# Masked queries by a GpSimd multiply instead of four DMAs, and the high query copies of the stack issued by ScalarE

## The chip, the cores and the metric

The kernel runs on one core of a Trainium2 chip. The metric is the time on the device in microseconds, lower is better. The core has five engines, each with its own list of instructions in a fixed order: TensorE (PE: matmuls), VectorE (DVE), ScalarE (ACT), GpSimd (POOL) and SyncE (SP), which here only issues DMAs. They wait for each other by semaphores. Every time is from a run on the chip or from a profile of one execution.

## The reference

A cross-attention layer and a feed-forward layer with 4-bit quantization, over a batch of 16. Inputs are x (16 x 224 x 512) and a context (16 x 750 x 512).

```python
def _L0_xattn_ref(q, k, v, Wq, bq, Wk, bk, Wv, bv, Wo, bo):
    qh, kh, vh = proj(q, Wq, bq), proj(k, Wk, bk), proj(v, Wv, bv)   # 16 heads of 32
    scores = jnp.einsum('bhqd,bhkd->bhqk', qh, kh) / math.sqrt(D_K)
    attn = jax.nn.softmax(scores, axis=-1)
    out = jnp.einsum('bhqk,bhkd->bhqd', attn, vh)
    return out.transpose(0, 2, 1, 3).reshape(B, -1, D_MODEL) @ Wo.T + bo

x = x + _L0_xattn_ref(_layernorm(x), ctx_1024, ctx_1024, ...)
gate, y = fp4_linear(ln, w_gate), fp4_linear(ln, w_up)               # ln = _layernorm(x)
x = x + fp4_linear(jax.nn.silu(gate) * y, w_down)
```

fp4_linear quantizes both operands in blocks of 16 and dequantizes them again before the product.

## The kernel before

Two stages follow each other: attention over all batches (the first 1650 us of the profile), then the feed-forward layer. The change lies in the attention.

The attention works through 64 slots, four per batch: a slot is a group t of 4 heads (HG = 4, 32 rows each, together 128 partitions) of one batch. Products are made exact by splitting each operand into a high part that TensorE takes whole and a low rest, and adding three products (PASSES, line 41).

For a group these steps are made, two slots ahead of its scores: the projected keys "k" (two halves) and queries "q" come from TensorE into a PSUM bank (lines 419 to 441); ScalarE copies the high part with the bias into k_part or q_part (lines 541 to 552), VectorE makes the low part (k_lo, q_lo, lines 621 to 637). There are two buffers of each by parity of t, only k_low is single.

One slot ahead, TensorE makes 16 "max" matmuls (line 473): the queries of one head against 375 keys each, whose row maximum VectorE takes (line 614). Since k_high holds 4 heads on its 128 partitions, the query operand must be zero outside the 32 rows of its head. It is q_masked, 128 x 4 x 224, whose block j holds the queries' high part on the rows of head j and zeros elsewhere. The zeros are written once at the start (line 727); the rows of the heads are copied for each group by four DMAs from q_part (line 788). The first max matmul waits for them (line 471). The negated maxima are transposed by TensorE ("shift", line 477) and copied by ScalarE into the last four rows of qstack (line 575).

For the scores a stack is made per head, so that one matmul over 100 rows does the three products and the shift: kstack holds the head's keys high, high, low and a row of ones, qstack the queries high, low, high and the shift. SyncE issues the copies: four for the low keys (line 796), then for each of the four heads two of high keys (line 802) and three of queries (line 805), 24 in all. The first score matmul of the group waits for all (lines 482 to 484).

Order: slot_units (line 177) gives every unit of work of a slot a place on a scale in which the 12 score matmuls of the slot stand at 0 to 11 (each a pair of matmuls, with an exponential on ScalarE of 128 x 448, line 539), and sorts. Each engine walks through the same sorted list and does what of each unit is its own, so an engine that waits holds up all its later units. Two score banks alternate: score n + 2 waits for exponential n. The places around the change, for group g + 1 in slot g: the low key copies 0.1, the other stack copies 0.12, max from 0.15 on, shift at about 9 and 11. For group g + 2: q at 7.12, 7.37, 6.6, 6.01 in slots 0 to 3, mask_q 0.05 after it. In slot 0 SyncE also loads the next batch's context and x at 2.6 (1500 and 448 KB, lines 773 and 777). In slot 2 ScalarE and VectorE split that context (ctx, places 0.15, 0.15, 1.88 and 2.49, lines 570 and 648) and the transposed x (0.38, 3.49). In slots 0, 1 and 3 VectorE quantizes a share of the feed-forward weights in 11 small steps (quantize_step, line 814); at places 7 to 10 these are steps with one or two SBUF inputs of 128 x 352 (lines 844 to 853).

The batches 1 to 14 are a loop on the engines (line 393), whose turn lies ahead of slot 0.

## Time and profile before

| | |
|---|---|
| Median of 3 runs | 2426.59 us (2416.27 to 2426.79) |
| The profiled execution | 2425.06 us, span 2423.2 us |
| TensorE busy (weight loads 1885.2) | 2240.0 us, 92% |
| VectorE busy | 1764.5 us, 73% |
| ScalarE busy | 844.4 us, 35% |
| GpSimd busy | 92.0 us, 4% |
| DMA, mean share of 16 engines | 29.8% on the queue of SyncE |
| Mean granted clock of TensorE | 0.969 of full speed |

The span is from the first to the last instruction, the time of an execution is slightly longer. Busy time doesn't count DMA issues: an engine that issues one is occupied and not busy. The clock is what the chip granted TensorE; 1.00 is 2.4 GHz and 0.50 is 1.2 GHz. A wait in the lists is idle time of an engine ahead of an instruction, with what ended it; "issue" is idle time that nothing the profile shows has ended.

### The profile page before, as it was taken

The numbers are of one execution on the slowest core, as the hardware profiler recorded it, in microseconds if no ns is written. First come the engines' busy times: TensorE is split into PE (matmuls) and PEld (weight loads), VectorE is DVE, ScalarE is ACT, GpSimd is POOL, SyncE is SP. The second block draws the span as 40 slices with busy tenths as digits, with TensorE's granted clock in tenths as the row PEclk, the third lists the DMA queues.
The fourth block names the chain that finished last, engine by engine and source line by source line (L and its number), as shares of the span: only waits on it lengthen the run. The fifth ranks groups of instructions, "written<-read, shape, count | busy, mean of one in ns | idle before, by whom it ended". The sixth has DMA issues, their size and how long they took to land. (4 is left out here: it accounts for less than half of the span.)

```text
span 2423.2 us, 50583 instructions
## 1 busy us (share of the span) xinstructions
PE 2240.0 (92%) x17444; PEld 1885.2 (78%) x17444; DVE 1764.5 (73%) x3102; ACT 844.4 (35%) x1677; POOL 92.0 (4%) x164
## 2 busy tenths in 40 slices
PE   4989899999998999999899999996799999999998
PEld 4778787787877877778778787864678888888887
DVE  4767667676666766757667676655899999999986
ACT  3444344443443434444344444434111111111111
POOL 0000000000000000000000000000000000000000
PEclk9999999999999999999999999998899999999999
DMA  4343434434334343443434434335000001010000
GB/s 152 107 120 80 120 89 115 118 89 117 94 110 120 83 117 90 114 123 81 117 90 114 123 82 117 92 89 163 31 27 30 36 26 39 26 39 26 35 18 27
DMA packets 136290, 204.74 MB, mean 84 GB/s; under 512 B 33872, under 2 KB 84560, under 8 KB 133568
## 3 DMA queue, kind: packets, MB, share of 16 engines
q1 hardware_dynamic: 136128, 202.22, 29.8%
q8 instruction: 146, 2.39, 0.4%
q14 instruction: 16, 0.13, 0.0%
HBM read 75.67 MB, written 23.33 MB: 41 GB/s over the span
## 5 line engine op out<-in xcount | busy, mean ns | idle before, releaser
L614 DVE TENSOR_REDUCE row_max<-max_bank 112x1 f32<-112x376 f32 (+1 forms) x1024 | 524.8, 542 | 478.0 <-PE max_bank L473 473.5
L539 ACT ACTIVATE probs<-score_bank 125x448 f32<-125x448 f32 x768 | 404.1, 542 | 315.2 <-PE score_bank L488 307.2
L473 PE MATMUL max_bank<-k_high,q_masked 128*112 128x376 f32 (+1 forms) x1024 | 321.1, 361 | 68.3 <-DMA q_masked<-q_part 55.4
L488 PE MATMUL score_bank<-qstack,kstack 100*128 100x224 f32 x1536 | 300.6, 282 | 27.8 <-issue 23.9
L488 PEld LDWEIGHTS score_bank<-qstack,kstack 100*128 100x128 f32 x1536 | 264.6, 191 | 60.0 <-issue 47.8
L473 PEld LDWEIGHTS max_bank<-k_high,q_masked 128*112 128x112 f32 x1024 | 163.9, 180 | 121.8 <-DMA q_masked<-q_part 52.8
L503 PE MATMUL pv_bank<-probs,values 125*32 125x224 f32 x3072 | 234.9, 379 | 9.2 <-ACT probs L539 9.2
L509 PE MATMUL pv_bank<-probs,ones 125*32 125x224 f32 x3072 | 232.5, 376 | 0.0
L1145 ACT ACTIVATE f_act_gate<-gate_bank 128x512 f32<-128x512 f32 (+1 forms) x84 | 47.3, 563 | 516.5 <-PE up_bank L1100 516.5
L1100 PE MATMUL gate_bank<-ffn_gate_hi,f_xqt 128*128 128x512 f32 (+1 forms) x672 | 218.9, 387 | 8.1 <-DVE f_xqt L1206 8.1
L447 PE MATMUL proj_bank<-wv_hi,ctx_hi 128*128 128x256 f32 x768 | 221.7, 289 | 4.3 <-DVE wo_lo L693 4.3
L447 PE MATMUL proj_bank<-wv_hi,ctx_lo 128*128 128x256 f32 x768 | 216.8, 282 | 0.0
L447 PE MATMUL proj_bank<-wv_lo,ctx_hi 128*128 128x256 f32 x768 | 216.7, 282 | 0.0
L1124 PE MATMUL down_bank<-ffn_down_hi,f_hqt 128*128 128x512 f32 x616 | 206.2, 401 | 6.6 <-DVE f_hqt L1222 6.6
L1100 PE MATMUL up_bank<-ffn_up_hi,f_xqt 128*128 128x512 f32 (+1 forms) x672 | 212.2, 377 | 0.0
L547 ACT ACTIVATE k_high<-proj_bank,biases 128x376 fp32r<-128x376 f32 (+1 forms) x128 | 73.5, 574 | 358.6 <-PE proj_bank L427 358.6
L427 PE MATMUL proj_bank<-ctx_hi,wk_hi 128*128 128x376 f32 (+1 forms) x512 | 176.2, 344 | 20.5 <-DVE ctx_lo L648 20.5
L427 PE MATMUL proj_bank<-ctx_lo,wk_hi 128*128 128x376 f32 (+1 forms) x512 | 173.9, 340 | 0.0
L427 PE MATMUL proj_bank<-ctx_hi,wk_lo 128*128 128x376 f32 (+1 forms) x512 | 172.6, 337 | 0.0
L447 PEld LDWEIGHTS proj_bank<-wv_hi,ctx_hi 128*128 128x128 f32 x768 | 147.7, 192 | 4.6 <-DVE wo_lo L693 4.6
L1100 PEld LDWEIGHTS gate_bank<-ffn_gate_hi,f_xqt 128*128 128x128 f32 x672 | 126.3, 189 | 27.9 <-DVE f_xqt L1206 8.5
L509 PEld LDWEIGHTS pv_bank<-probs,ones 125*32 125x32 f32 x3072 | 105.3, 116 | 53.5 <-issue 12.0
(119 smaller groups left out, 4035.5 us busy)
## 6 DMA issues: line engine op xcount, KB each, us to landing
kstack<-k_high SPq DMA_DIRECT2D x512, 93.8 KB, 2.2
ctx_raw<-in_ctx SPq DMA_DIRECT2D x16, 1500.0 KB, 7.0
kstack<-k_low SPq DMA_DIRECT2D x256, 93.8 KB, 2.2
qstack<-q_part SPq DMA_DIRECT2D x768, 28.0 KB, 1.9
ffn_quant<-fw_share SPq DMA_DIRECT2D x48, 176.0 KB, 1.9
fw_raw<-ffn_quant SPq DMA_DIRECT2D x33, 256.0 KB, 4.1
xn<-in_x SPq DMA_DIRECT2D x16, 448.0 KB, 8.0
q_masked<-q_part SPq DMA_DIRECT2D x256, 28.0 KB, 1.9
```

The lines of the kernel that those rows point to most:

```text
L427: last = nc.tensor.matmul(out[:, 0:hi - lo], w_hi_lo[W_K][ws][:, c, g * P:(g + 1) * P], ctx_part[cs][:, c, lo:hi], start=(n == 0), stop=(n ...
L447: last = nc.tensor.matmul(out[:, 0:256], ctx_part[cs][:, c, kt * KW:kt * KW + P], w_hi_lo[W_V][ws][:, c, half * 256:(half + 1) * 256], sta ...
L473: nc.tensor.matmul(out[0:QH, 0:hi - lo], q_masked[t % 2][:, j, half * QH:(half + 1) * QH], k_part[t % 2][0][:, lo:hi], start=True, stop=Tr ...
L488: last = nc.tensor.matmul(score_bank[j % 2][:, k * SQ:(k + 1) * SQ], kstack[t % 2][0:STK, j, kt * KW:kt * KW + P], qstack[t % 2][:, j, :], ...
L503: last = nc.tensor.matmul(pv_bank[t % 2][j * DK:(j + 1) * DK, 0:SQ], values[:, t % NG // 2, kt, col:col + DK], probs[p][:, j, k, :], start ...
L509: last = nc.tensor.matmul(pv_bank[t % 2][j * DK:(j + 1) * DK, SQ:2 * SQ], ones[0:KW, :], probs[p][:, j, k, :], start=False, stop=(kt == KT ...
L539: nc.scalar.activation(probs[p][:, j, :, :], score_bank[j % 2][0:KW, 0:2 * SQ].rearrange("p (k q) -> p k q", k=2), ACT.Exp, scale=float(DK ...
L547: nc.scalar.activation(k_part[t % 2][0][:, lo:hi], src[:, 0:hi - lo], ACT.Identity, bias=biases[:, 1, t % NG:t % NG + 1]).then_inc(hi_done ...
L614: nc.vector.tensor_reduce(row_max[:, half, j, kh:kh + 1], mbank[0:QH, 0:KSPLIT[kh + 1] - KSPLIT[kh]], AX.X, ALU.max).then_inc(max_reduced, 1)
L1100: last = nc.tensor.matmul(banks[par][:, 0:w], xqt[n % 2][xs_][:, kc, :], ffn[m][ws][:, kc, chunk(c)], start=(k == 0), stop=(k == 11))
L1124: last = nc.tensor.matmul(down_bank[n % 2][:, :], hqt[hs][:, m, :], ffn[2][ws][:, m, :], start=(m == 0 and k == 0), stop=(m == FC - 1 and ...
L1145: nc.scalar.activation(act_gate[par][:, 0:w], gate_bank[par][:, 0:w], ACT.Silu).then_inc(silu_done, 1)
```

## The change

GpSimd makes q_masked: one multiply of q_part, repeated over the four blocks, with head_mask, a 128 x 4 tensor of ones and zeros that VectorE sets at the start, repeated over the 224 columns. It waits for ScalarE's high part and for the last max matmul of two slots ago. The zeroing at the start goes, and with it SyncE's wait. The eight copies of the queries' high part into qstack leave SyncE's list; a new unit stack_q(j) of group g + 1 stands at 1.5, 3.5, 5.5 and 7.5 in slot g, and at each ScalarE issues the two copies of head j. They count on semaphores of their own: the first score waits for them too, and ScalarE waits for them before it writes the next queries into the same buffer. SyncE keeps 4 low key, 8 high key and 4 low query copies per slot. At the start the eight copies of group 0 stand between "stack" and the split of Wv.

```diff
+STACK_Q = (1.5, 3.5, 5.5, 7.5)
...
         add(0.12, ("stack", g + 1))
+        add(STACK_Q, *[("stack_q", g + 1, j) for j in range(HG)])
...
-    units += [("stack_low", 0), ("stack", 0), ("split_w", 2)]
+    units += [("stack_low", 0), ("stack", 0)] + [("stack_q", 0, j) for j in range(HG)] + [("split_w", 2)]
...
-    STACK_DMAS = 5 * HG
+    STACK_DMAS = 3 * HG
... (TensorE, max)
-                        reached(pe, masked[t % 2], mask_count(b, t))
+                        reached(pe, masked, count(b, "q", t))
... (TensorE, score)
                         reached(pe, stacked[t % 2], stack_count(b, t))
+                        reached(pe, q_stacked[t % 2], q_stack_count(b, t))
... (ScalarE)
                 elif kind == "q":
                     act.wait_ge(made["q"], count(b, *u))
+                    reached(act, q_stacked[t % 2], q_stack_count(b, t - 2))
...
+                elif kind == "stack_q":
+                    par = t % 2
+                    if u[2] == 0:
+                        act.wait_ge(hi_done["q"], count(b, "q", t))
+                        reached(act, made["score"], count(b, "score", t - 2, 2, 3))
+                    j = u[2]
+                    for r in (0, 2):
+                        act.dma_start(qstack[par][heads_of[r], j, :].bitcast(F32),
+                                      q_part[par][0][heads_of[j], :].bitcast(F32)).then_inc(q_stacked[par], 16)
... (VectorE, at the start)
+        nc.vector.memset(head_mask[:, :], 0.0).then_inc(head_mask_made, 1)
+        dve.wait_ge(head_mask_made, 1)
+        for j in range(HG):
+            nc.vector.memset(head_mask[j * DK:(j + 1) * DK, j:j + 1], 1.0).then_inc(head_mask_made, 1)
... (GpSimd)
+                elif kind == "mask_q":
+                    pool.wait_ge(hi_done["q"], count(b, "q", t))
+                    reached(pool, made["max"], count(b, "max", t - 2, 15))
+                    nc.gpsimd.tensor_tensor(q_masked[t % 2][:, :, :],
+                                            q_part[t % 2][0][:, :].unsqueeze(1).to_broadcast([P, HG, SQ]),
+                                            head_mask[:, :].unsqueeze(2).to_broadcast([P, HG, SQ]), ALU.mult)\
+                        .then_inc(masked, 1)
...
-            nc.gpsimd.memset(q_masked[par][:, :, :].bitcast(F32), 0.0).then_inc(mask_zeroed, 1)
... (SyncE)
-                elif kind == "mask_q":
-                    sp.wait_ge(hi_done["q"], count(b, "q", t))
-                    reached(sp, made["max"], count(b, "max", t - 2, 15))
-                    for j in range(HG):
-                        sp.dma_start(q_masked[t % 2][heads_of[j], j, :].bitcast(F32),
-                                     q_part[t % 2][0][heads_of[j], :].bitcast(F32)).then_inc(masked[t % 2], 16)
...
-                        for r, qp in enumerate((0, 1, 0)):
-                            sp.dma_start(qstack[par][heads_of[r], j, :].bitcast(F32),
-                                         q_part[par][qp][heads_of[j], :].bitcast(F32)).then_inc(stacked[par], 16)
-
-        sp.wait_ge(mask_zeroed, 2)
+                        sp.dma_start(qstack[par][heads_of[1], j, :].bitcast(F32),
+                                     q_part[par][1][heads_of[j], :].bitcast(F32)).then_inc(stacked[par], 16)
```

## Rows read from the trace of the kernel before

**Rows 1.** Page, part 1: busy us, share of the span, instructions.

```profile
PE 2240.0 (92%) x17444; PEld 1885.2 (78%) x17444; DVE 1764.5 (73%) x3102; ACT 844.4 (35%) x1677; POOL 92.0 (4%) x164
```

**Rows 2.** List of waits, whole span: total us, times, longest.

```profile
PE max_bank L473 <- DMA q_masked<-q_part: 55.4, 16, 6.8
```

**Rows 3.** TensorE's timeline: start us, us, instruction [idle before <-releaser].

```profile
34.26 0.94 PE L473 MATMUL max_bank<-k_high,q_masked 128*112 128x376 f32 x2 [4.36 <-DMA q_masked<-q_part]
...
480.89 0.59 PE L473 MATMUL max_bank<-k_high,q_masked 128*112 128x376 f32 x2 [0.94 <-DMA q_masked<-q_part]
...
879.53 0.26 PE L477 MATMUL max_bank<-ident,neg_max 112*128 112x112 f32 x1
...
881.61 0.48 PE L488 MATMUL score_bank<-qstack,kstack 100*128 100x224 f32 x2
...
885.71 0.97 PE L473 MATMUL max_bank<-k_high,q_masked 128*112 128x376 f32 x2 [3.62 <-DMA q_masked<-q_part]
...
920.66 0.59 PE L503 MATMUL pv_bank<-probs,values 125*32 125x224 f32 x8 [0.61 <-ACT probs L539]
```

**Rows 4.** SyncE's timeline in slot 0 of batch 8.

```profile
862.86 1.87 SPq L805 DMA_DIRECT2D qstack<-q_part  x3
...
875.79 0.34 SPq L773 DMA_DIRECT2D ctx_raw<-in_ctx  x1
...
876.94 2.71 SPq L788 DMA_DIRECT2D q_masked<-q_part  x4
```

**Rows 5.** DMA issues by tile: count, KB each, median us to landing.

```profile
ctx_raw<-in_ctx SPq DMA_DIRECT2D x16, 1500.0 KB, 7.0
```

**Rows 6.** The four copies into q_masked issued from 876 to 881.

```profile
DMA to landing us min/median/max: 6.4/6.7/6.9
```

**Rows 7.** Windows behind slot 1's wait: busy us, then granted clock, DMA share, GB/s.

```profile
480.90:488.90 8.00, 8.00 (x65) 6.40 (x66) 4.63 (x12) 1.44 (x3) 1.48 (x4) 1.00 0.48 123
...
885.70:893.70 8.00, 7.99 (x55) 5.73 (x56) 2.81 (x8) 0.78 (x2) 0.74 (x2) 0.67 0.35 92
```

**Rows 8.** Windows at the start of slot 0, batches 4 and 5.

```profile
456.50:462.50 6.00, 5.92 (x50) 3.82 (x51) 2.00 (x4) 1.09 (x2) 0.00 (x0) 0.72 0.48 127
554.20:560.20 6.00, 5.92 (x60) 4.71 (x61) 3.00 (x7) 2.17 (x5) 0.00 (x0) 1.00 0.49 127
```

**Rows 9.** TensorE's timeline: first score of slot 0 in batches 2, 4, 5, 14.

```profile
253.86 0.47 PE L488 MATMUL score_bank<-qstack,kstack 100*128 100x224 f32 x2 [1.55 <-issue]
...
456.58 0.48 PE L488 MATMUL score_bank<-qstack,kstack 100*128 100x224 f32 x2 [2.32 <-issue]
...
554.24 0.48 PE L488 MATMUL score_bank<-qstack,kstack 100*128 100x224 f32 x2 [2.36 <-issue]
...
1463.69 0.48 PE L488 MATMUL score_bank<-qstack,kstack 100*128 100x224 f32 x2 [1.89 <-issue]
```

**Rows 10.** GpSimd's instructions by line: busy us, mean ns | idle before.

```profile
L720 POOL TENSOR_TENSOR res<-res,bo_rows 112x512 f32<-112x512 f32 x32 | 42.7, 1354 | 1007.2 <-DMA res<-in_x 1007.2
```

**Rows 11.** Timeline of all engines around 752.7.

```profile
752.25 0.53 DVE L853 SCALAR_TENSOR_TENSOR fw_share<-fw_power,fw_share 128x352 f32<-128x352 f32 x1
...
752.70 1.28 POOL L720 TENSOR_TENSOR res<-res,bo_rows 112x512 f32<-112x512 f32 x1 [62.52 <-DMA res<-in_x]
...
752.81 1.55 DVE L854 TENSOR_TENSOR fw_share<-fw_share,fw_scale 128x352 f32<-128x352 f32 x1
```

**Rows 12.** VectorE's timeline in slot 0 of batch 8.

```profile
876.98 0.34 DVE L844 TENSOR_SCALAR fw_power<-fw_power 128x352 f32<-128x352 f32 x1
...
878.92 0.16 DVE L619 TENSOR_REDUCE neg_max<-row_max 112x4 f32<-112x8 f32 x1
```

**Rows 13.** ScalarE's timeline in slot 2 of batch 8.

```profile
917.20 0.55 ACT L539 ACTIVATE probs<-score_bank 125x448 f32<-125x448 f32 x1
917.62 0.84 ACT L570 ACTIVATE ctx_hi<-ctx_raw 128x750 fp32r<-128x750 f32 x1
918.92 0.54 ACT L539 ACTIVATE probs<-score_bank 125x448 f32<-125x448 f32 x1 [0.45 <-PE score_bank L488]
```

More of the change, by code:

```diff
@@ L275, in attention @@
     ones = sb("ones", [P, DK])
+    head_mask = sb("head_mask", [P, HG])
     biases = sb("biases", [P, 3, KC])
@@ L338, in attention @@
     neg_zeroed = sem("neg_max_zeroed")
-    mask_zeroed = sem("q_mask_zeroed")
-    masked = [sem(f"q_masked{i}") for i in range(2)]
+    head_mask_made = sem("head_mask_made")
+    masked = sem("q_masked")
+    q_stacked = [sem(f"q_high_stacked{i}") for i in range(2)]
     fw_loaded = sem("fw_share_loaded")
@@ L351, in attention @@
     fw_stored = sem("fw_share_stored")
-    STACK_DMAS = 5 * HG
+    heads_of = [slice(j * DK, (j + 1) * DK) for j in range(HG)]
+    STACK_DMAS = 3 * HG
     def index_of(unit, b):
@@ L370, in stack_count, with q_stack_count @@
         return (b * (NG // 2) + t // 2 + 1) * 16 * STACK_DMAS
-    def mask_count(b, t):
-        return (b * (NG // 2) + t // 2 + 1) * 16 * HG
+    def q_stack_count(b, t):
+        return (b * (NG // 2) + t // 2 + 1) * 16 * 2 * HG
     def low_count(b, t):
@@ L725, in _ @@
             nc.gpsimd.memset(kstack[par][0:SHIFT, :, SK:SKP].bitcast(F32), 0.0).then_inc(pads_zeroed, 1)
-        for par in range(2):
-            nc.gpsimd.memset(q_masked[par][:, :, :].bitcast(F32), 0.0).then_inc(mask_zeroed, 1)
         for part in ctx_part:
@@ L734, in _ @@
         pool.wait_ge(small_loaded, 64)
+        pool.wait_ge(head_mask_made, 1 + HG)
         phases(pool, body)
@@ L742, in share_of @@
                 bass.ds(b, 1), :, :].rearrange("b p k -> (b p) k")
-        heads_of = [slice(j * DK, (j + 1) * DK) for j in range(HG)]
         def rows(tensor, b, h=None):
```

## The prediction

> **What bounds the kernel now.** I read the page's engine table first: TensorE is busy for 2240.0 us of 2423.2 [rows 1], so what counts is what makes TensorE stand still and at which clock it then runs. I went to the list of waits next. The largest wait of TensorE that recurs is the maximum matmul's, for the masked queries that a DMA writes: 55.4 us in 16 waits, the longest 6.8 [rows 2]. TensorE's timeline says where they are: one of 4.36 us at the start, 0.94 us in batch 4, 3.62 us in batch 8 [rows 3]. The sixteen are the one at the start and one in each of batches 1 to 15, always at the first maximum matmul of slot 1, and none in slots 0, 2 and 3.
>
> The reason stands in SyncE's issue rows of slot 0 [rows 4]. Three copies of a stack take 1.87 us to issue, 0.62 us each, and SyncE issues 24 such copies per slot before it comes to anything else. So the context load, placed at 2.6, is issued only at 875.79, and the four mask copies, 876.94 to 879.65, right behind it. A context load lands 7.0 us after its issue [rows 5]; these four mask copies landed 6.4 to 6.9 us after theirs, the last at about 885.7 [rows 6], which is when TensorE went on.
>
> The clock is the second part. The stretches of 8 us behind the waits have the granted clock: 0.67 behind the 3.62 us of batch 8, 1.00 behind the 0.94 us of batch 4 [rows 7]. I took that view for all 14 waits of batches 1 to 14: twelve ran at 0.61 to 0.79 and two at 1.00, together 27.8 us of granted clock lost, TensorE dropping to its 1.2 GHz level after standing idle and coming back to 2.4 GHz. A like fall follows the loop's turn at the start of slot 0: in 8 of 13 batches the first 6 us have 0.72, in 5 of them 1.00, as in [rows 8].
>
> **What is removed.** Per slot four mask copies and eight query-stack copies leave SyncE, 12 x 0.62 = 7.4 us of its issue time [rows 4]. The masked queries no longer stand behind the context load. What that gives I take from the starts of slot 0 [rows 9]: from 253.86 to 1463.69 are 12 batches, 100.82 us each. Batch 4 (456.58 to 554.24) took 97.66 us with a wait of 0.94 and no fall of the clock behind it: 96.72 without the wait. But it began with a fall (0.72 over 6 us, 1.68 us lost) which 5 in 13 lack, so a mean quiet batch is 96.72 - 1.68 x 5/13 = 96.07 us. The saving is 4.75 us per batch, 66.5 us over 14, and 0.8 us more for the short wait of the last batch. From above it is bounded by waits and lost clock added, 55.4 - 4.4 + 27.8 = 79 us; from below by batch 4 as it is, 4.1 x 14 = 57. I take 67.
>
> **The mask on GpSimd.** No row shows a GpSimd multiply of 896 columns. The nearest is its addition of 512 columns, 1354 ns in the mean [rows 10]; by columns that is 2.4 us, and the undisturbed ones of 1.26 us give 2.2. I take 2.3; the ends are 1.3 (no dearer than 512 columns) and 4.6 (twice, for the two spread operands). In slot 0 ScalarE has the queries at 876.0 (SyncE could issue their copies from 876.94 on), so the mask is ready at 878.3; it is wanted at 885.71 - 3.62 = 882.1, so even 4.6 us is covered. Its price is on VectorE. When GpSimd's addition began at 752.70, VectorE's multiply of two SBUF tensors beside it took 1.55 us, where the like step just before took 0.53 [rows 11]: it waited for GpSimd. In slot 0 the mask (876.0 to 878.3) meets VectorE's quantizer step of 876.98 [rows 12], which then starts at 878.3, 1.3 us late; behind it in VectorE's order are a second step, two row maxima and the negated maximum of 878.92, and TensorE's transpose of 879.53 [rows 3] waits for that last one. That maximum ended at 879.1; with the hop between engines the slack is about 0.3 us, so TensorE loses 1.0 us. In slot 1 the same pair of steps meets the mask with more slack, I put a quarter of that price; in slots 2 and 3 no step with two SBUF inputs runs then. 1.25 x 16 batches = 20 us; ends 0 (all in slack) and 40 (4.6 us masks).
>
> The Trainium skill states this as a lock (SBUF — State Buffer, "SBUF: two separate sides"): GpSimd and VectorE share one port pair, and an operation of VectorE with two SBUF inputs or in a 2-port mode blocks fully while a GpSimd operation has it. The row of 1.55 us agrees for two inputs; if one-input steps were free, as the rule does not have it, only the step behind it would be late, and slot 0 would lose about 0.7 instead of 1.0 us.
>
> **The query stack on ScalarE's queue.** No row shows a DMA issued by ScalarE. I price it as on SyncE, 0.62 us, in which ScalarE does nothing else: 1.24 us per pair. The low end is nothing. Four pairs are 5 us per slot of about 24; at most places ScalarE idles that long. Slot 2 is different, for ScalarE also splits the next context there, and TensorE already waits 0.61 us for its exponential at 920.66 [rows 3]. ScalarE's rows [rows 13]: exponential 1 ends at 917.75; the first pair comes then and ends at 919.0; context part 2 (0.84) and exponential 2 follow, at 919.8 instead of 918.92; the part and the exponential behind move by the same 0.87 us. So TensorE's wait grows to 1.5 us. The second pair (place 3.5) comes after the exponential that TensorE waits for and delays nothing that is late. But SyncE is still issuing its 16 copies (10 us) when pairs one and two come; if issues disturb each other for half their time the first pair costs 0.6 us more. I take 1.5 us per batch, 15 batches with a next context: 22 us; ends 0 and, at 2.5 us per pair, 2.1 us and more (below). Nothing waits for a pair to land but the next slot's first score: the last pair (place 7.5) is issued near 877, lands after some 2 us outside a load.
>
> **The rest.** With 8 copies fewer ahead of it the context load goes out 5.0 us earlier, near 870.8; the burst, 9.9 us from its issue to the last landing at 885.7, is over near 880.7, ahead of slot 1 (881.6) by 0.9 us. ScalarE's new wait before the queries is for copies of two slots ago, long landed; the five small memsets are before the first load arrives. At the start the mask saves 2 us of the 4.36 us wait, but eight issues (5 us) now stand before the split of Wv on ScalarE, which VectorE wants before its first row maximum: +2 us net (ends -2 and +5).
>
> **Sum.** 2425.06 us (the profiled execution) - 66.5 - 0.8 + 22 + 20 + 2 = 2402 us. The execution lies 0.06% under the median of 2426.59, so the sum stands for the median too. A change of this kernel under 0.5% (12 us) can't be told from none.
>
> **Rivals.** (B) The prices hide: an issue on ScalarE is short, and VectorE's late steps fall into slack. With 0.5 us per batch left of both (8 us) that is 2425 - 67 + 2 + 8 = 2368 us. For it speaks that ScalarE was idle for 0.45 us ahead of its exponential of 918.92, waiting for TensorE [rows 13]; against it that TensorE waits for ScalarE 1.7 us later all the same.
>
> (C) Slower: ScalarE becomes the bound in slot 2. If an issue of ScalarE has to queue behind one of SyncE each time, a pair takes 2.5 us; exponential 3 is then 2.1 us late, TensorE stands for 2.7 us in one piece, and behind idle pieces of that kind the clock lost at least 1.7 us. 3.8 x 15 = 57 us, and the total is 2425 - 67 + 57 + 22 = 2437; with 0.5 us in each of the other slots too (22 us) it is 2459 us. It decides against the change from 3.0 us per batch on ((67 - 22) / 15), a pair of about 1.9 us with the fall of the clock. Against it: SyncE's own issues follow each other at 0.62 us without gaps, and no row has two issuers.
>
> The Trainium skill has the rule behind this (Perfetto Trace Analysis, "DMA Instruction — HWDGE"): the block that generates descriptors is locked for one sequencer at a time, and the lock wait is part of the instruction. No run here shows it so far.
>
> (D) The wait moves: pairs three and four of slot 0 are now in flight with the context load, and slot 1's first score waits for them as the mask was waited for. If SyncE is slowed and loads at 873, the burst ends at 883 and 1.5 to 2 us of wait with its clock fall stay: half of the gain, 2402 + 33 = 2435 us.
>
> (E) The mask is late on GpSimd for a reason of its own, an operation over 5.7 us: 2425 + 20 + 22 = 2467 us or so.
>
> **Chances.** Forecast 0.44, B 0.18, C 0.20, D 0.13, E 0.05. The forecast's own range is 2385 to 2420. The range for 8 in 10 takes in most of B and the lower half of C: 2362 to 2448. Faster by over 0.5% (under 2414): most of the forecast and all of B, 0.57. Within 0.5%: the forecast's tail, D and a little of C, 0.21. Slower: most of C, part of D, and E, 0.22.
>
> **What would show it.** Right: no wait of the maximum matmul for q_masked beyond the first, granted clock 1.00 in slot 1, batches of about 98.8 us; ctx_raw issued some 5 us earlier in slot 0; VectorE's step beside the mask over 1.5 us long; TensorE's wait for the exponential of slot 2 at 1.2 to 2 us. Wrong: pairs over 2 us on ScalarE, or 0.7 and less in the clock column behind 920; a wait of the score for qstack at slot 1; a mask over 3 us.

## The result, and the profile after

The changed kernel takes 2360.41 us in the median of four runs (2359.93 to 2364.39), the kernel before, run beside it, 2423.48 (2416.27 to 2426.79): a ratio of 0.9747, 95% interval 0.972 to 0.9775. It is 63 us faster. The forecast was 2402 with a range of 2362 to 2448, so the direction was right and the size was not: the gain is more than twice the 23 us predicted. In all the fences below, rows between those shown are left out, also where no dots stand.

The first lines of the changed kernel's page have each engine's busy time; they answer to [rows 1].

```profile
span 2358.6 us, 50604 instructions
PE 2215.0 (94%) x17444; PEld 1872.2 (79%) x17444; DVE 1782.2 (76%) x3107; ACT 848.6 (36%) x1677; POOL 194.5 (8%) x226
```

TensorE does the same 17444 matmuls in 25 us less, GpSimd is busy for 102 us more, VectorE for 18 us more. The list of waits (total us, times, longest) answers to [rows 2]:

```profile
PE max_bank L478 <- DVE row_max L630: 16.1, 22, 5.5
PE pv_bank L509 <- ACT probs L545: 10.7, 20, 0.7
PE max_bank L482 <- DVE neg_max L635: 6.1, 15, 1.2
PE score_bank L494 <- ACT probs L545: 4.5, 14, 0.7
```

The 55.4 us for q_masked are gone; of them one wait of 2.39 us is left, at the start, on GpSimd. What came in its place is small: neg_max 6.1 us in 15 waits, and probs a little more often than before. TensorE's timeline of the changed kernel (start, duration, instruction, idle before it) gives the batches, against [rows 3, 9]:

```profile
29.80 0.40 PE L478 MATMUL max_bank<-k_high,q_masked 128*112 128x376 f32 x1 [2.39 <-POOL q_masked L740]
37.97 0.66 PE L478 MATMUL max_bank<-k_high,q_masked 128*112 128x376 f32 x1 [5.54 <-DVE row_max L630]
65.11 0.45 PE L494 MATMUL score_bank<-qstack,kstack 100*128 100x224 f32 x2 [1.03 <-ACT qstack L582]
...
249.13 0.48 PE L494 MATMUL score_bank<-qstack,kstack 100*128 100x224 f32 x2 [2.05 <-issue]
828.02 0.48 PE L494 MATMUL score_bank<-qstack,kstack 100*128 100x224 f32 x2 [1.87 <-issue]
847.71 0.29 PE L482 MATMUL max_bank<-ident,neg_max 112*128 112x112 f32 x1 [0.35 <-DVE neg_max L635]
1401.96 0.48 PE L494 MATMUL score_bank<-qstack,kstack 100*128 100x224 f32 x2 [1.94 <-issue]
1594.12 0.69 PE L929 MATMUL fw_bank<-ident,fw_raw 128*128 128x128 f32 x2 [6.23 <-DMA fw_raw<-ffn_quant]
```

From 249.13 to 1401.96 are 12 batches of 96.07 us; they were 100.82. The start is 3.0 us longer (first score at 65.11 instead of 62.11), and the first matmul after attention comes at 1594.12 instead of 1661.13, 67 us earlier. Behind it the rest takes 2 us longer than before, 764.5 against 762.1.

The rows of windows (start:end, length, busy time by engine, granted clock, DMA share, GB/s) are the beginning of slot 1 of batch 8, and the beginning of slot 0 of two batches; they answer to [rows 7, 8].

```profile
851.00:859.00 8.00, 8.00 (x70) 6.71 (x59) 4.85 (x14) 2.00 (x5) 1.48 (x4) 1.00 0.56 139
...
249.13:255.13 6.00, 6.00 (x51) 4.22 (x52) 2.10 (x4) 1.09 (x2) 0.00 (x0) 0.72 0.55 140
347.37:353.37 6.00, 5.97 (x60) 4.75 (x61) 3.01 (x7) 2.20 (x5) 0.00 (x0) 1.00 0.59 143
```

Slot 1 runs at the full clock now, and so does everything but the beginning of slot 0: in batches 2 to 13 each stretch of 6 us behind the first has a granted clock of 1.00. Behind the loop's turn the clock still falls, but in 4 of 13 batches, where it was 8 of 13. Each such fall costs 1.6 us (in the kernel e1 below, called mask-only, six batches that begin with one take 96.23 us in the mean, six without 94.65).

The timelines of SyncE and of the mask show what moved, against [rows 4, 11, 12]. The first two lines are SyncE and GpSimd in slot 0 of batch 8, the others VectorE there and in slot 1.

```profile
838.23 0.37 SPq L797 DMA_DIRECT2D ctx_raw<-in_ctx  x1
843.93 1.68 POOL L740 TENSOR_TENSOR q_masked<-q_part,head_mask 128x896 fp32r<-128x896 f32 x1 [23.35 <-ACT q_part L558]
...
844.31 0.44 DVE L650 SCALAR_TENSOR_TENSOR q_part<-proj_bank,biases,q_part 128x224 fp32r<-128x224 f32 x1
844.67 1.14 DVE L860 TENSOR_SCALAR fw_power<-fw_power 128x352 f32<-128x352 f32 x1
847.40 0.16 DVE L635 TENSOR_REDUCE neg_max<-row_max 112x4 f32<-112x8 f32 x1
...
867.62 0.33 DVE L860 TENSOR_SCALAR fw_power<-fw_power 128x352 f32<-128x352 f32 x1
869.56 1.24 DVE L862 SCALAR_TENSOR_TENSOR fw_power<-fw_share,fw_power 128x352 uint32<-128x352 uint32 x1
```

The context load goes out 10.2 us into the slot (838.23 - 828.02); it was 17.0 (875.79 [rows 4] less 858.81, the first score of that slot), so it is 6.8 us earlier where I had 5.0. The mask takes 1.68 us, each of the 64 between 1678 and 1682 ns, and is ready at 845.61, some 4.6 us before slot 1 wants it (its first maximum matmul starts at 850.20). The quantizer step L860 takes 1.14 us beside it and 0.33 alone (the row of 867.62); in slot 1 the next mask (868.74 to 870.42) holds step L862 in the same way, 1.24 us where it takes 0.53 alone.

ScalarE's timeline in slot 2 shows the issues (ACTq), against [rows 13]:

```profile
878.69 0.52 ACTq L591 DMA_DIRECT2D qstack<-q_part  x1
878.74 0.54 ACT L569 ACTIVATE xt_part<-proj_bank 128x448 fp32r<-128x448 f32 x1
879.16 0.55 ACT L545 ACTIVATE probs<-score_bank 125x448 f32<-125x448 f32 x1
879.25 1.40 ACTq L591 DMA_DIRECT2D qstack<-q_part  x1
880.69 0.83 ACT L577 ACTIVATE ctx_hi<-ctx_raw 128x750 fp32r<-128x750 f32 x1 [0.98 <-issue]
881.43 0.53 ACT L545 ACTIVATE probs<-score_bank 125x448 f32<-125x448 f32 x1
```

The issue of 878.69 and the activations of 878.74 and 879.16 run at the same time, and the issue of 879.25 begins while the exponential executes: what ScalarE really loses to this pair is 0.98 us, although the pair's issues add up to 1.92.

### The profile page after: what moved, and what is told of

Its sections match the earlier page's. It is cut to its first block and busy times, and to the rows that moved or that the text cites. A ratio compares the mean times of both kernels' runs of the same rounds, so it can differ in the third digit from the quotient of the medians.

```text
span 2358.6 us, 50604 instructions
## 1 busy us (share of the span) xinstructions
PE 2215.0 (94%) x17444; PEld 1872.2 (79%) x17444; DVE 1782.2 (76%) x3107; ACT 848.6 (36%) x1677; POOL 194.5 (8%) x226
## 3 DMA queue, kind: packets, MB, share of 16 engines
q8 instruction: 146, 2.39, 0.5%
## 5 line engine op out<-in xcount | busy, mean ns | idle before, releaser
L545 ACT ACTIVATE probs<-score_bank 125x448 f32<-125x448 f32 x768 | 411.7, 544 | 386.1 <-PE score_bank L494 293.9
L478 PE MATMUL max_bank<-k_high,q_masked 128*112 128x376 f32 (+1 forms) x1024 | 312.6, 353 | 20.4 <-DVE row_max L630 16.1
L509 PE MATMUL pv_bank<-probs,values 125*32 125x224 f32 x3072 | 224.1, 364 | 11.1 <-ACT probs L545 10.7
L515 PE MATMUL pv_bank<-probs,ones 125*32 125x224 f32 x3072 | 219.4, 358 | 0.0
L740 POOL TENSOR_TENSOR q_masked<-q_part,head_mask 128x896 fp32r<-128x896 f32 x64 | 107.6, 1681 | 1202.6 <-ACT q_part L558 1092.9
```

Of the source, the lines that this page charges most:

```text
L478: nc.tensor.matmul(out[0:QH, 0:hi - lo], q_masked[t % 2][:, j, half * QH:(half + 1) * QH], k_part[t % 2][0][:, lo:hi], start=True, stop=Tr ...
L509: last = nc.tensor.matmul(pv_bank[t % 2][j * DK:(j + 1) * DK, 0:SQ], values[:, t % NG // 2, kt, col:col + DK], probs[p][:, j, k, :], start ...
L515: last = nc.tensor.matmul(pv_bank[t % 2][j * DK:(j + 1) * DK, SQ:2 * SQ], ones[0:KW, :], probs[p][:, j, k, :], start=False, stop=(kt == KT ...
L545: nc.scalar.activation(probs[p][:, j, :, :], score_bank[j % 2][0:KW, 0:2 * SQ].rearrange("p (k q) -> p k q", k=2), ACT.Exp, scale=float(DK ...
L740: nc.gpsimd.tensor_tensor(q_masked[t % 2][:, :, :], q_part[t % 2][0][:, :].unsqueeze(1).to_broadcast([P, HG, SQ]), head_mask[:, :].unsquee ...
```

## Experiments

All ratios are against the kernel before, run beside each group of four. In every group its median was between 2420.76 and 2427.27 us.

**What makes the gain.** The theory after the result: the masked queries no longer land behind the context load, and that is all of it. Three kernels reach it in three ways; the changed kernel stood beside them.

> The changed kernel once more, beside the three halves of it, so that all four have the same runs of the kernel before. 2360 us, 64 under the kernel before; 12 batches of 96.0 us each, and no wait of a maximum matmul for q_masked after the start.

Measured: 2356.40 us (2351.51 to 2365.87), 0.9738 (0.9712 to 0.9764); batches of 95.77 us in the profile, where 96.0 were expected. Differences to the changed kernel are taken from this 2356.4 below.

```diff
 e1: the changed kernel, all stack copies issued by SyncE
-        add(STACK_Q, *[("stack_q", g + 1, j) for j in range(HG)])
...
-    STACK_DMAS = 3 * HG
+    STACK_DMAS = 5 * HG
...
-                        sp.dma_start(qstack[par][heads_of[1], j, :].bitcast(F32), ...
+                        for r, qp in enumerate((0, 1, 0)):
+                            sp.dma_start(qstack[par][heads_of[r], j, :].bitcast(F32), ...
```

> GpSimd builds the masked queries, but all 24 stack copies stay with SyncE. Theory T (the whole gain is that the masked queries no longer land behind the context load; the added ScalarE issues cost about 0.5 us per batch in slot 2 and 3 us at the start): the gain is whole and the price of the issues falls away, 2350 us (2342 to 2362). Rival R1 (the lighter queue of SyncE, whose context load goes out 6.8 us earlier, carries part of the gain): the context load stays at 17 us into slot 0, and part of the gain is missing, 2375 to 2400. Rival R2 (the costs are as large as predicted, 1.5 us per batch for the issues, and hidden by something gained elsewhere): 2335 us or less.

Measured: 2343.01 us (2341.57 to 2347.35), 0.9683 (0.966 to 0.9707). The context load still goes out 16.8 us into slot 0 (830.29 - 813.54). As theory T says, the gain is whole without SyncE's relief (against R1), and the ScalarE half of the change is not part of it but a price: 13.4 us. R2 fails too, which wanted a larger price.

```diff
 e2: the kernel before, with the eight copies on ScalarE's queue and no mask on GpSimd
+STACK_Q = (1.5, 3.5, 5.5, 7.5)
...
+        add(STACK_Q, *[("stack_q", g + 1, j) for j in range(HG)])
...
+                    for r in (0, 2):
+                        act.dma_start(qstack[par][heads_of[r], j, :].bitcast(F32), ...
```

> ScalarE's queue issues the eight copies of the queries' high part, and SyncE still writes the masked queries with four copies. The context load goes out near 10 us into slot 0 instead of 17, its burst of 10 us ends at 20 us, the mask copies are issued from 17.2 us on and are wanted at 23.3. Theory T: the masked queries land ahead of that, the wait is gone by this edit alone, and the issues cost their 0.5 us per batch: 2366 us (2355 to 2380). Rival R3 (only GpSimd takes the wait away, since the mask copies still run into the burst's last third): the wait stays at 1 us or more with a fall of the clock in half of the batches, 2385 to 2410. As predicted (22 us for the issues, 20 for the lock, no mask on GpSimd here): 2425 - 67 + 22 + 2 = 2382.

Measured: 2369.89 us (2369.16 to 2375.81), 0.9794 (0.977 to 0.9819). T had 2366, R3 2385 and more: this half alone takes the wait away as well. Its only wait for q_masked is the 4.36 us of the start. In slot 0 the context load is issued at 839.32, the four mask copies at 843.09, and these land in 4.8 to 5.4 us; they were 6.4 to 6.9 [rows 6]. They are still held up, but in time. Another wait appears in their place, which belongs to rival D below: in nine batches the first score of slot 1 waits for the query stack.

```profile
PE score_bank L497 <- DMA qstack<-q_part: 8.5, 9, 1.5
```

```diff
 e3: the kernel before, with one place changed
-        add((at["load"],) * 2, ("load_ctx", 1), ("load_x", 1))
+        add((8.0, at["load"]), ("load_ctx", 1), ("load_x", 1))
```

> The kernel before with one number changed: the context load (not the one of x) has place 8.0 instead of 2.6 in slot 0, behind the four mask copies (place 7.17) in SyncE's order. Nothing moves to another engine. Theory T: the mask copies, issued near 876, land some 2 to 3 us later and not 6.9, the wait of slot 1 is gone, and the time is that of quiet batches without any added cost: 2425 - 67 = 2358 us (2345 to 2368). Rival R1 (what counts is SyncE's relief, or GpSimd's mask being ready at 1.7 us): SyncE comes to the mask copies no earlier than 875.8, and the wait only shortens, 2385 to 2424. Rival R4 (the load, now near 878.5, makes slot 1 wait for its stack instead): about 2424 or more.

Measured: 2356.41 us (2354.75 to 2357.28), 0.9732 (0.9709 to 0.9755), the time of the whole change. SyncE's timeline in slot 0 of its batch 7, against [rows 4]:

```profile
744.97 2.43 SPq L788 DMA_DIRECT2D q_masked<-q_part  x4
747.66 0.35 SPq L773 DMA_DIRECT2D ctx_raw<-in_ctx  x1
```

The same four copies, issued at the same place of the slot but ahead of the load, land in 1.8 to 2.9 us. Theory T is shown: one number in the order of SyncE's queue is worth 65.6 us, and neither another engine (R1) nor less work is needed; slot 1's stack was not late (R4). The 65.6 are net. Behind the start, three waits for q_masked are left (2.10, 0.24 and 0.48 us), and three matmuls wait 2.8 us in all for k_low, whose writer VectorE waits for the low key copies issued behind the load.

**What the issues on ScalarE cost.**

```diff
 e5: the changed kernel, each of ScalarE's copies issued again into a spare buffer
+                        act.dma_start(spare[par][heads_of[j], r // 2, :],
+                                      q_part[par][0][heads_of[j], :].bitcast(F32)).then_inc(q_stacked[par], 16)
```

> The changed kernel with each of ScalarE's eight copies per slot issued a second time into a spare buffer (as many bytes again, in the same places): pairs become fours, 2.3 us instead of 1.16. Theory T (a pair costs 0.4 us per batch because only its end sticks out from under the running activation; a second pair has no such cover): slot 2 pays 1.2 us more, the other slots a little, the start 5 us: 2356 + 5 + 18 = 2379, 2370 to 2400. Rival P0 (ScalarE's issues hide in idle time whatever their number): 2361. Rival P2 (the predicted C: fours bound ScalarE in slot 2 and the clock falls behind the wait, 3.8 us per batch): 2418 or more.

Measured: 2492.25 us (2486.14 to 2503.37), 1.0289 (1.0259 to 1.032): 136 us more than the changed kernel, far above T (2370 to 2400) and P0. P2 had "2418 or more", and is right in kind and too small in size: it had 3.8 us more per batch, where 8.7 were measured (104.16 against 95.5 us in batches that begin without a fall of the clock). 22 us more come before batch 2, whose slot 0 starts at 271.33 instead of 249.13. The list of waits and slot 2 of one batch, first ScalarE, then TensorE:

```profile
PE score_bank L495 <- ACT probs L546: 63.3, 55, 2.1
PE max_bank L479 <- ACT qstack L583: 30.8, 40, 1.2
...
951.65 0.55 ACT L546 ACTIVATE probs<-score_bank 125x448 f32<-125x448 f32 x1
951.74 1.34 ACTq L594 DMA_DIRECT2D spare<-q_part  x1
953.11 0.61 ACTq L592 DMA_DIRECT2D qstack<-q_part  x1
954.41 0.83 ACT L578 ACTIVATE ctx_hi<-ctx_raw 128x750 fp32r<-128x750 f32 x1 [2.21 <-issue]
955.72 0.48 PE L495 MATMUL score_bank<-qstack,kstack 100*128 100x224 f32 x2 [1.44 <-ACT probs L546]
```

Each pair has become a four: its first issue (951.19 to 951.70, not shown) and a third of its second hide under activations, and the rest stands bare: ScalarE is idle for 2.21 us in one piece, and TensorE waits 1.44 us for the exponential. Its list of waits has 94 us for ScalarE in these two rows; behind some of them the clock falls (in eight batches of twelve a stretch of 6 us in the first half of slot 2 has 0.55 to 0.85, where the changed kernel has 1.00). By arithmetic ScalarE would still have had room: it executes activations for 11.1 us of a slot (44.41 us in the batch from 828.02 to 923.65), and 16 issues add 10 us to that, in a slot of 26. It isn't its sum that decides but which exponential stands behind a group of issues. So the predicted rival C, ScalarE as the bound, is real; it begins at fours, not at pairs.

```diff
 e6: the changed kernel, slot 2's pairs behind the context parts
-        add(STACK_Q, *[("stack_q", g + 1, j) for j in range(HG)])
+        add((5.5, 6.7, 7.5, 9.5) if g == 2 else STACK_Q, *[("stack_q", g + 1, j) for j in range(HG)])
```

> The changed kernel with the four pairs of slot 2 at 5.5, 6.7, 7.5 and 9.5 instead of 1.5, 3.5, 5.5 and 7.5, behind the four context parts that ScalarE splits there. Theory T (what the issues cost in a batch is in slot 2, between 1.5 and 3.5, where ScalarE is late for the exponential): 0.3 to 0.5 us per batch come back, 2350 us (2346 to 2353). Rival P3 (the cost is spread over all slots, by SyncE's and ScalarE's issues holding each other up): 2356, as the changed kernel. Rival P4 (the last pair, issued near 9.5, lands too late for the first score of slot 3): 2362 or more, with waits for qstack there.

Measured: 2362.96 us (2360.55 to 2366.44), 0.9757 (0.9732 to 0.9781), not faster, against T. TensorE's waits of a pv matmul for probs grow to 20.9 us in 30 (they were 10.7 in 20), one of them 0.74 us in slot 2's second half, while the scores' waits for probs shrink to 1.9 us in 6 (from 4.5 in 14): the price moved with the pairs. No wait for qstack shows, so P4's cause is absent, though the time is its time. Both orders of slot 2 that were tried cost about as much.

```diff
 e8: the changed kernel, start
-    units += [("stack_low", 0), ("stack", 0)] + [("stack_q", 0, j) for j in range(HG)] + [("split_w", 2)]
+    units += [("stack_low", 0), ("stack", 0)] + [("split_w", 2)] + [("stack_q", 0, j) for j in range(HG)]
```

> The changed kernel with one thing moved in the start: ScalarE's part of the split of Wv comes before its eight copies of slot 0's queries and not behind them. Mask-only started slot 0 at 58.3 us and the changed kernel at 65.1 to 65.4, so the eight issues cost the start 7 us. Theory S (they do it through the split of Wv, which VectorE waits for ahead of its first row maximum): the wait of 5.5 us behind row_max goes, the first score comes at 60 to 62, 2352 us (2349 to 2354). Rival S0 (the start is bound by the copies landing, or by SyncE's issues held up beside ScalarE's): it stays at 65, 2356.

Measured: 2350.77 us (2348.1 to 2355.39), 0.9695 (0.9658 to 0.9732). The wait of 5.54 us behind row_max is gone and the first score comes at 58.65 us; in mask-only, without any of these issues, at 58.31. The two kernels' ScalarE in the start, the changed one first:

```profile
27.93 5.24 ACTq L591 DMA_DIRECT2D qstack<-q_part  x8
33.22 1.91 ACT L601 ACTIVATE wv_hi<-probs 128x2048 fp32r<-128x2048 f32 x1 [5.32 <-issue]
```
```profile
28.28 1.90 ACT L601 ACTIVATE wv_hi<-probs 128x2048 fp32r<-128x2048 f32 x1
28.41 5.25 ACTq L591 DMA_DIRECT2D qstack<-q_part  x8
```

Eight issues of 5.24 us ahead of the split cost 6.5 us or more; behind it they cost the start 0.3. Theory S holds.

**What the lock costs.**

```diff
 e4: the changed kernel, the mask written twice
+                    reached(pool, masked, 2 * count(b, "q", t) - 1)
+                    nc.gpsimd.tensor_tensor(q_masked[t % 2][:, :, :], ... , ALU.mult).then_inc(masked, 1)
```

> The changed kernel with GpSimd writing each mask twice, one behind the other (the second writes the same values): GpSimd holds what it shares with VectorE for 3.4 us instead of 1.68 in every slot. Theory T (the lock is real, and what makes it cheap is that the mask ends 0.35 us behind VectorE's slack in slot 0): the 1.7 us more are paid in full in slot 0 and in part in slot 1, 1.7 to 2.5 us per batch, 27 to 40 us: 2392 us (2380 to 2400). Rival L0 (VectorE's steps beside the mask lie in slack, the lock costs TensorE nothing at any length of this size): 2356 to 2364. If the masked queries at 3.4 us came too late for TensorE, a wait of the maximum matmul for q_masked would show, which T doesn't expect (they are wanted 6 us after the queries).

Measured: 2398.93 us (2394.37 to 2402.88), 0.9901 (0.9875 to 0.9928), 42 us above the changed kernel, as theory T says (2380 to 2400); L0 fails. The waits for neg_max have 25 us of it (31.2 in 27 waits, they were 6.1 in 15); falls of the clock have some of the rest, at the loop's turn (8 of 13) and in the middle of four batches.

```diff
 e11: e4, with three quantizer steps of slot 0 moved behind the negated maximum
-        "ffn_quant": (3.25, 4.97, 6.08, 6.45, 7.12, 8.21, 8.35, 9.18, 9.62, 10.0, 10.54),
+        "ffn_quant": (3.25, 4.97, 6.08, 6.45, 7.12, 9.18, 9.19, 9.2, 9.62, 10.0, 10.54),
```

> The kernel that writes each mask twice (2399 us, 42 above the changed kernel, with 1.7 us of wait for neg_max in slot 0) with the same three quantizer steps moved behind the negated maximum. Theory Q (the price of the long mask is the lock, and it falls only on the steps whose operands are all in SBUF; what reads PSUM runs beside the mask at full speed): with no such step beside it in slot 0 most of the 42 us goes, 2366 us (2360 to 2374), slot 1's share stays. Rival Q2 (a longer mask slows VectorE's row maxima too, or lands too late): 2385 or more.

Measured: 2357.96 us (2353.97 to 2362.7), 0.972 (0.9682 to 0.9758), just under Q's range of 2360 to 2374: with these steps moved the doubled mask is as cheap as the single one with the steps in their old places. Of the 41 us some 8 are falls at the turn (3 in place of 8). Slot 1's share stays, 3.8 us in 11 waits for neg_max. The timelines of slot 0, VectorE and GpSimd of e4, and TensorE's transpose, then the same of e11:

```profile
859.76 1.68 POOL L740 TENSOR_TENSOR q_masked<-q_part,head_mask 128x896 fp32r<-128x896 f32 x1 [21.67 <-ACT q_part L558]
861.52 1.68 POOL L745 TENSOR_TENSOR q_masked<-q_part,head_mask 128x896 fp32r<-128x896 f32 x1
860.51 1.13 DVE L865 TENSOR_SCALAR fw_power<-fw_power 128x352 f32<-128x352 f32 x1
861.68 1.91 DVE L867 SCALAR_TENSOR_TENSOR fw_power<-fw_share,fw_power 128x352 uint32<-128x352 uint32 x1
864.63 0.16 DVE L635 TENSOR_REDUCE neg_max<-row_max 112x4 f32<-112x8 f32 x1
864.93 0.29 PE L482 MATMUL max_bank<-ident,neg_max 112*128 112x112 f32 x1 [1.73 <-DVE neg_max L635]
```
```profile
841.21 1.68 POOL L740 TENSOR_TENSOR q_masked<-q_part,head_mask 128x896 fp32r<-128x896 f32 x1 [23.85 <-ACT q_part L558]
842.97 1.68 POOL L745 TENSOR_TENSOR q_masked<-q_part,head_mask 128x896 fp32r<-128x896 f32 x1
841.60 0.44 DVE L650 SCALAR_TENSOR_TENSOR q_part<-proj_bank,biases,q_part 128x224 fp32r<-128x224 f32 x1
842.66 1.00 DVE L630 TENSOR_REDUCE row_max<-max_bank 112x1 f32<-112x376 f32 x2 [0.62 <-PE max_bank L478]
843.79 0.16 DVE L635 TENSOR_REDUCE neg_max<-row_max 112x4 f32<-112x8 f32 x1
```

In e4 both quantizer steps are held, by 0.80 and 1.38 us, 2.18 in all; TensorE waits 1.73. In the changed kernel one step is held by 0.81 and TensorE waits 0.35. Both give the same slack, 0.45 us. In e11 VectorE's operations that read PSUM run beside the mask at their usual durations, and so does the negated maximum, which reads and writes SBUF: 0.16 us, from 843.79, while the second mask lasts to 844.65. Slot 0's transpose doesn't wait. Theory Q is shown, but for one thing: what is held are the quantizer's steps, and not every operation with its operands in SBUF.

The same move made to mask-only:

> Mask-only (2343 us) with VectorE's quantizer steps 6 to 8 of slot 0 at 9.18, 9.19 and 9.2 instead of 8.21, 8.35 and 9.18: step 6 is the one that took 1.06 us beside the mask, and all three now stand behind the negated maximum. Theory Q (the lock's whole price in slot 0 runs through this step): the 0.27 us wait of the transpose for neg_max goes, 4 us in all, 2339 us (2335 to 2342). Rival Q1 (seven steps in a row then make VectorE late for the end of slot 0): 2346 or more.

Measured: 2341.20 us (2333.32 to 2343.39), 0.9643 (0.9605 to 0.9681), inside Q's range. The waits for neg_max are gone from the list, but the clock fell behind the loop's turn in 10 of 13 batches (6 in mask-only), and the intervals of the two overlap: no difference can be told. These two are the fastest kernels, and both are faster than the changed one.

**Rival D, the query stack behind the load.**

```diff
 e7: the changed kernel, place of both loads
-        add((at["load"],) * 2, ("load_ctx", 1), ("load_x", 1))
+        add((6.5,) * 2, ("load_ctx", 1), ("load_x", 1))
```

> The changed kernel with the loads of the context and of x at place 6.5 instead of 2.6 in slot 0, so that they are issued some 16 us into the slot, as in the kernel before, and their burst of 10 us ends at about 26, past the start of slot 1 (22.8). The masks are GpSimd's and don't care. Theory D (the prediction's rival: pairs three and four of the query stack, at 5.5 and 7.5, land behind the burst, and slot 1's first score waits for them as the masks were waited for): 1.5 to 2 us of wait with its fall of the clock, 33 us: 2380 to 2395, and a wait of the score for qstack in each batch. Rival D0 (a copy issued in the burst's second half lands in time, or pair four only is late, by less than 1 us): 2356 to 2368.

Measured: 2356.95 us (2352.37 to 2360.0), 0.973 (0.9705 to 0.9755). It tells nothing of D: the load went out 10.66 us into the slot (833.98 - 823.32), as before. A place in SyncE's list delays only what has a waiting unit ahead of it, and since the masks left the list there is none between 2.6 and 6.5.

```diff
 e9: the changed kernel, SyncE waits for slot 2's queries before the loads, which have place 7.3
+                    if t:
+                        sp.wait_ge(hi_done["q"], count(b, "q", 2))
```

> The changed kernel with a true delay of the context load: the run that set it to place 6.5 issued it no later (10.7 us into slot 0 instead of 10.2), since SyncE has nothing to wait for in between. Here SyncE waits for slot 2's queries before both loads, so they are issued some 16 us into the slot and are in flight until 25, past the start of slot 1 at 22.8. Theory D2 (prediction's rival D in small, as seen in the stack-only run, where the first score of slot 1 waited 1.26 us for qstack with the clock at 1.00 behind it): the last pair lands 0.3 to 1.2 us late, 5 to 18 us in all, 2361 to 2374. Rival D (as predicted: 1.5 to 2 us of wait with its fall of the clock): 2385 to 2395. Rival D0 (the pairs are issued ahead of the load and don't care): 2354 to 2360.

Measured: 2376.47 us (2366.63 to 2380.3), 0.9801 (0.9763 to 0.9838). It lies between D2 (2361 to 2374) and D (2385 to 2395). The load is issued 16 us into the slot; the wait is there, in 10 batches, by its row in the list and in batch 8:

```profile
PE score_bank L494 <- DMA qstack<-q_part: 8.3, 10, 1.9
853.39 0.36 PE L494 MATMUL score_bank<-qstack,kstack 100*128 100x224 f32 x1 [0.73 <-DMA qstack<-q_part]
```

So D's wait exists, at half its predicted length (0.83 us in the mean, where I had 1.5 to 2), and without its fall of the clock: slot 1 has 1.00 in all twelve batches looked at. The kernel is 20 us slower than the changed one, and these waits explain only the profiled execution, at 2366.63 us the fastest of the five; what the other four add is open. With the load at 10.2 us, in the changed kernel, the wait doesn't occur. In stack-only, where the load goes out at 12.0 us (839.32 - 827.32) with four mask copies behind it, it does (8.5 us, above).

## Why the prediction was wrong

**What was right.** The bound (TensorE's wait for the masked queries, with the clock fall behind it), its cause (the copies stand behind the context load), and its price: 67.3 us predicted, 65.6 measured in e3, which changes nothing else. That they are so close is in part luck: e3 still has 2.8 us of waits for the mask, 2.8 for k_low, and two falls at the turn more than before (3 us), so the wait alone was worth some 74. The short mask was in time everywhere (against E). The start was predicted at +2 and measured at +3.0, by larger parts than I gave: the mask saves 3.8 us (62.11 to 58.31 in mask-only) and the issues cost 6.8.

**First failed step: the query stack on ScalarE's queue, 22 us in the batches.** I wrote that an issue takes 0.62 us, "in which ScalarE does nothing else", and added whole pairs to the chain of exponentials. The duration was right: 607 ns in the median, 513 to 1900. The exclusion was wrong: an issue begins while the activation ahead of it executes. In slot 2 TensorE waits 0.67 us for the exponential behind the first pair, and 0.21 at a score; before it waited 0.61 [rows 3]. That is 0.27 us more in the place for which I had 0.9 to 1.5. All places together: batches without the falls of the clock take 95.5 us in the changed kernel (96.07 less 4 falls of 1.6 in 12 batches) and 94.65 in mask-only, so 0.85 us per batch, 13 us. The collisions with SyncE were rightly feared, and they are in the trace (1.40 us on ScalarE at 879.25, 1.31 us on SyncE at 879.33), but only now and then: ScalarE's 512 issues in attention sum to 319 us, 0.62 each.

The Trainium skill's rule (Perfetto Trace Analysis, "DMA Instruction — HWDGE") says that an issue may have to wait for the block that generates the descriptors, and that this lies inside the instruction. The two rows of 1.3 to 1.4 us agree; had it held for every pair, as in C, the time would have been 2437 us.

**Second failed step: the mask on GpSimd, 20 us for the lock.** The mechanism was right, in step and engine. Two sizes were off, the mask (1.68 us where I took 2.3 by columns of an addition) and the slack (0.45 us where I had 0.3). A delay of 0.81 less 0.45 leaves the 0.35 us that TensorE waits, in place of 1.0; the quarter more for slot 1 did not show. The row of neg_max in the list has 6.1 us in 15 waits, so the term is 5 to 6 us instead of 20. It was small because the slack covered more than half of the delay, and e4 shows what the next 1.7 us cost, 42.

The Trainium skill (SBUF — State Buffer, "SBUF: two separate sides") has the lock as exclusive, for VectorE's operations with two SBUF inputs or in a 2-port mode. The rows agree, and they decide what I had left open in the prediction: the one-input step L860 is held too (0.33 to 1.14).

**Third: the falls at the loop's turn.** My quiet batch of 96.07 us held 8 falls in 13, as before. It came out at 96.07 by luck: from 94.7 (e3's 95.89 less 9 falls of 1.6 in 12 batches) plus the prices, with 4 falls. The 94.7 is arithmetic; e3's three batches without a fall take 95.98, and two of them hold the waits for k_low. Against e3, where the clock fell in 10 of 13 batches, that is some 10 us that no term had. e3 also has 3 us of waits for k_low and 3 for the mask that the changed kernel hasn't.

**The sum as measured.** 2422 (before) - 65.6 + 13 (issues) + 5 (lock) + 3 (start) - 10 (fewer falls than e3) - 3 (k_low) - 3 (the mask's waits left in e3) = 2361 us, where 2356 to 2360 was timed. Two terms of 42 us together were really 18, and that is what put rival B (the prices hide, 2368 us) ahead of my forecast. B was nearest by luck too: it had 8 us for both prices, and the falls, which it didn't name, made up for the rest. I gave it 0.18, since I held TensorE's wait of 0.61 us in slot 2 against it. That row says that ScalarE is late there, but not that an issue makes it later.

**Left open.** Why the clock falls behind the loop's turn in 2 to 10 of 13 batches. The kernels in which SyncE issues all stack copies have 8 (before), 6 (mask-only), 10 (its moved form) and 10 (e3); those in which ScalarE issues its part have 2 to 5, except the doubled mask with 8. So the second half of the change may give back a few us at the turn of what it costs elsewhere; that is not shown. The idle time of the turn, 1.5 to 2.6 us, doesn't tell the two cases apart: in the changed kernel the clock fell behind 1.59 us and held behind 2.13. Since only one execution of each is profiled, the counts may partly be chance.

## What to carry to other kernels

When a small copy is late, look first at what its queue issued just before it, and try the order before anything else: here one place number gave as much as moving twelve copies to two engines. A price that is added to an engine counts only beyond what the running instruction covers and beyond the slack behind it, so find both in the timeline, and the point where they end: pairs of issues cost 0.85 us per batch and fours 8.7 more; a mask of 1.7 us cost 0.35 and one of 3.4 us five times that. And where a change has two halves, time each alone: the second half here made the first one 13 us worse.

## What the hardware showed that I had not expected

- A DMA issued by ScalarE starts under the running activation, as in slot 0 of batch 8 of the changed kernel. Eight in a row take 5.24 us, and the activation behind them waits for all.

```profile
831.27 0.55 ACT L545 ACTIVATE probs<-score_bank 125x448 f32<-125x448 f32 x1 [2.09 <-PE score_bank L494]
831.42 1.17 ACTq L591 DMA_DIRECT2D qstack<-q_part  x2
```

- The mask on GpSimd, 128 x 896 with both operands repeated, takes 1.68 us, 1.9 ns per column; its addition of 128 x 512 columns in 1.26 us had 2.5 [rows 10, 11].
- Beside GpSimd's mask, VectorE's operations that read PSUM keep their durations (0.44, and 1.00 for two row maxima), and so does the small reduce from SBUF to SBUF that makes the negated maximum (0.16). The quantizer's steps, all in SBUF, stand until the mask ends, with one input (0.33 to 1.14 us) as with two (0.53 to 1.24).
- Four small copies issued behind a 1500 KB load land in 6.4 to 6.9 us (1.2 us behind it [rows 4, 6]) or 4.8 to 5.4 (3.8 us behind it, stack-only), those issued 2.7 us ahead of it in 1.8 to 2.9 (e3).
